# Pair scores as matmuls of 512 columns, with the halves of the sum added on VectorE

## What is computed

```python
scores = einsum('bsd,bmd->bsm', layernorm(x), ctx) / sqrt(1024)   # 8 x 1024 x 64
scores = where(mask, scores, -1e30)
x = x + where(any(mask), einsum('bsm,bmd->bsd', softmax(scores), ctx), 0)

y = layernorm(x)                                  # 8 x 1024 x 1024
base = einsum('btd,od->bto', y, weight)           # 1024 x 1024
probs = softmax(einsum('btd,ed->bte', y, router_w))     # 8 experts
w_dense = the two largest probs, normed to a sum of 1, zero elsewhere
Ax = einsum('nd,erd->ner', y, lora_A)             # rank 16
x = x + base + 2.0 * einsum('ner,ne,eor->no', Ax, w_dense, lora_B)
```

## Time and profile before

| | us |
|---|---|
| median of 3 runs | 981.63 |
| lowest and highest | 981.21, 981.75 |
| the profiled execution's own time | 982.01 |
| its span | 980.1 |

### The profile page before, as it was taken

One profiled execution on the slowest core, in us unless ns is written; L12 is line 12 of the kernel. 1 busy time (PEld: TensorE's weight loads), 2 busy tenths in 40 slices (PEclk: granted clock), 3 DMA queues, 4 the chain that ended last, 5 costly groups with the idle time before them and its releaser, 6 DMA issues.

```text
span 980.1 us, 18830 instructions
## 1 busy us (share of the span) xinstructions
PE 972.0 (99%) x6081; PEld 960.0 (98%) x6081; DVE 851.1 (87%) x2201; ACT 471.6 (48%) x930; POOL 141.2 (14%) x278
## 2 busy tenths in 40 slices
PE   8999999999999999999999999999999999999998
PEld 7999999999999999999999999999999999999998
DVE  6989988899988998989988899888999889888774
ACT  7755544445444455435444445454454444444420
POOL 3311111111111111111111111111111111111110
PEclk9999999999999999999999999999999999999999
DMA  8646666656576566575656665666765576665532
GB/s 323 230 130 156 160 169 161 186 137 161 151 177 188 146 130 157 162 203 150 162 127 158 202 159 154 140 154 176 178 151 158 124 192 167 161 161 125 123 71 71
DMA packets 156096, 156.62 MB, mean 160 GB/s; under 512 B 93968, under 2 KB 128912, under 8 KB 156048
## 3 DMA queue, kind: packets, MB, share of 16 engines
q1 hardware_dynamic: 137616, 138.63, 52.0%
q10 hardware_dynamic: 18432, 17.45, 9.5%
HBM read 78.74 MB, written 33.55 MB: 115 GB/s over the span
## 4 chain that ended last, share of the span: by engine, by line
PE 94%; DVE 3%; DMA 1%; issue 1%; ACT 1%; POOL 0%; SPq 0%; DVEq 0%; ACTq 0%; POOLq 0%
PE base_ps L1119 27%; PE base_ps L1120 27%; PE base_ps L1121 27%; PE ro_ps L1193 3%; PE ro_ps L1194 3%; PE s_ps L1148 3%; PE s_ps L1146 3%; PE base_ps L1225 1%; DMA xq<-xn 1%; DVE stats L913 1%; DVE x2T L929 0%; DVE w_raw L907 0%; DMA ctxT_raw<-in_ctxT 0%; DVE ctx_sum L790 0%; PE s_ps L1156 0%
## 5 line engine op out<-in xcount | busy, mean ns | idle before, releaser
L1119 PE MATMUL base_ps<-w_hi,xT_hi 128*128 128x392 f32 x1512 | 495.6, 328 | 0.8 <-DVE xT_lo L936 0.8
L1120 PE MATMUL base_ps<-w_lo,xT_hi 128*128 128x392 f32 x1512 | 494.4, 327 | 0.0
L1121 PE MATMUL base_ps<-w_hi,xT_lo 128*128 128x392 f32 x1512 | 494.4, 327 | 0.0
L1119 PEld LDWEIGHTS base_ps<-w_hi,xT_hi 128*128 128x128 f32 x1512 | 285.8, 189 | 2.8 <-issue 1.0
L1120 PEld LDWEIGHTS base_ps<-w_lo,xT_hi 128*128 128x128 f32 x1512 | 285.8, 189 | 1.6
L1121 PEld LDWEIGHTS base_ps<-w_hi,xT_lo 128*128 128x128 f32 x1512 | 285.8, 189 | 0.0
L929 DVE STREAM_TRANSPOSE x2T<-xq 128x512 f32<-128x512 f32 x122 | 166.5, 1472 | 18.1 <-DMA xq<-xn 18.0
L495 POOL TENSOR_TENSOR rstd<-var_eps,neg_half 128x1 f32<-128x1 f32 x64 | 61.7, 964 | 391.4 <-DVE var_eps L920 391.4
L622 ACT CAST xT_hi<-x2T 128x512 fp32r<-128x512 f32 x122 | 69.5, 617 | 99.0 <-DVE x2T L929 99.0
L936 DVE TENSOR_TENSOR xT_lo<-x2T,xT_hi 128x512 fp32r<-128x512 f32 x122 | 78.3, 683 | 0.0
L610 ACT ACTIVATE xn<-w_raw,shift,rstd 128x1024 f32<-128x1024 f32 x32 | 39.7, 1241 | 77.3 <-POOL shift L498 77.3
(11 more groups left out here) (132 smaller groups left out, 1389.8 us busy)
## 6 DMA issues: line engine op xcount, KB each, us to landing
xT_raw<-in_xT SPq DMA_DIRECT2D x62, 512.0 KB, 5.3
w_raw<-in_x SPq DMA_DIRECT2D x32, 512.0 KB, 3.5
out<-x_first SPq DMA_DIRECT2D x32, 512.0 KB, 2.9
out<-w_raw SPq DMA_DIRECT2D x31, 512.0 KB, 2.8
xq<-xn SPq DMA_DIRECT2D x122, 128.0 KB, 4.1
xq<-xn ACTq DMA_DIRECT2D x122, 128.0 KB, 4.1
x_first<-in_x SPq DMA_DIRECT2D x30, 512.0 KB, 3.6
h<-w_raw SPq DMA_DIRECT2D x248, 16.0 KB, 1.8
```

The lines of the kernel that those rows point to most:

```text
L1119: pe.matmul(out_, a_hi, w_h, start=start, stop=False, skip_group_check=again)
L1120: pe.matmul(out_, a_hi, w_l, start=False, stop=False, skip_group_check=again)
L1121: return pe.matmul(out_, a_lo, w_h, start=False, stop=stop, skip_group_check=again)
```

## The change

The scores' two matmuls per chunk become one: the moving operand is the high and the low part of both tiles, 512 columns, through `xT_parts`, and the result fills the whole bank `s_ps`, the products of the high part in its first half, those of the low part in its second. The two halves, which the accumulation in PSUM added before, are now added by VectorE: a VectorE operation is given only one operand in PSUM here, so ScalarE first copies the second half to `s_low` in SBUF, VectorE adds it to the first half into `s_sum`, and the transpose reads `s_sum`. The first tiles, whose scores go other ways (`first_scores`, `first_pair_scores`), stay as they are; 29 pairs are changed. Apart from that the loads of the next batch's context leave step 1: `load_ctxT` goes to step 0 and `load_ctx` to step 2.

```diff
@@ SyncE, step
-                if j == 1 and exists((b, TPB)):
+                if j == 0 and exists((b, TPB)):
+                    sp.wait_ge(ctxT_split, b + 1)
+                    load_ctxT(b + 1)
+                if j == 2 and exists((b, TPB)):
                     sp.wait_ge(ctx_split, b + 1)
                     sp.wait_ge(mask_step, b * 3 + 3)
                     load_ctx(b + 1)
-                    sp.wait_ge(ctxT_split, b + 1)
-                    load_ctxT(b + 1)
@@ ScalarE
+            def s_low_copy(tile):
+                act.wait_ge(sT_done, pairs(tile, 1, 1))
+                act.copy(s_low, s_ps[:, T2:2 * T2]).then_inc(s_low_copied, 1)
...
                 if h_is_late(tile):
                     hT_high(tile)
+                if j % 2 == 1 and exists(after(tile, 3)) and not turned_on_pe(after(tile, 3), 6):
+                    s_low_copy(after(tile, 3))
                 if exists(nxt):
                     x2T_high(nxt)
@@ VectorE, s_transposes
-                dve.wait_ge(sT_done, pairs(tile, 1, 1))
+                dve.wait_ge(s_low_copied, pairs(tile, 1, 1 - 3))
+                dve.tensor_tensor(s_sum, s_ps[:, 0:T2], s_low, ALU.add).then_inc(s_sum_done, 1)
+                dve.wait_ge(s_sum_done, pairs(tile, 1, 1 - 3))
                 dve.transpose(sq.rearrange("p (j k c) -> p k j c", k=2, c=QP),
-                              s_ps[:, 0:T2].rearrange("p (j c k) -> p k j c", k=2, c=QP)).then_inc(sq_done, 1)
+                              s_sum.rearrange("p (j c k) -> p k j c", k=2, c=QP)).then_inc(sq_done, 1)
@@ TensorE, pair_scores
                 for c in range(C):
-                    pe.matmul(s_ps[:, 0:T2], ctxT[:, c, :], xT_hi[:, :, c, :].rearrange("p t n -> p n t"),
-                              start=(c == 0), stop=False)
-                    mm = pe.matmul(s_ps[:, 0:T2], ctxT[:, c, :], xT_lo[:, :, c, :].rearrange("p t n -> p n t"),
-                                   start=False, stop=(c == C - 1))
+                    mm = pe.matmul(s_ps[:, :], ctxT[:, c, :], xT_parts[:, :, :, c, :].rearrange("p k t n -> p k n t"),
+                                   start=(c == 0), stop=(c == C - 1))
```

More of the change, by code:

```diff
@@ L196, in xattn_lora_moe_kernel @@
         sq = w_raw[0][:, C - 2, 0:T2]
+        s_sum = w_raw[0][:, C - 4, 0:T2]
+        s_low = w_raw[0][:, C - 5, 0:T2]
         s_raw = w_raw[0][:, C - 3, 0:T2].rearrange("p (i k c) -> p i k c", i=Q, k=2)
@@ L324, in xattn_lora_moe_kernel @@
         e_loaded = sem("e_loaded")
+        s_low_copied = sem("s_low_copied")
+        s_sum_done = sem("s_sum_done")
         sq_done = sem("sq_done")
```

## The result

| | before | after |
|---|---|---|
| median, range of 4 runs, us | 981.64 (981.21 to 981.75) | 995.92 (995.84 to 996.37) |
| profiled execution, its span | 982.01, 980.1 | 995.95, 994.2 |

The ratio is 1.0145, 95% interval 1.0133 to 1.0158. The change costs 14.3 us; 995.7 was forecast. The granted clock is 1.0 in both.

A forecast was written before the change was run, and what follows sets the result against it. TensorE, busy 99%, was taken as the bound, with little margin before its readouts. Matmuls -1.5, stalls +16.1, old waits -0.5 give +14.1 on 982.01: 996.1, or 995.7 us as median; range 987 to 1003.

The forecast's parts named there:

- The mechanism: From scores to next even readout, the path has 0.36 us margin; the added delay makes TensorE stall in 29 pairs.
- ordinary: 15 pairs at neither special place: path 13.42 against TensorE's 13.78; 0.54 us idle plus 0.10 restart each, 9.6 us.
- with the mean: 7 pairs in whose window TensorE also issues the context's mean: 0.31 us idle plus 0.10 restart each, 2.9 us.
- The first tiles of a batch: 7 pairs whose path ends at a new batch's first tile, VectorE about 0.1 late: 0.52 us each, 3.6 us.
- The delay itself: Copy and add move the transpose's start after the scores from +0.03 to +0.88, 0.85 us, all arriving at the path's end.
- rival 3: Unseen path slack, say where e transfers land: nothing waits, only -1.5 us stays, 980.1; decides at 0.5 slack; chance 0.08.
- The matmuls: Scores on TensorE: eight matmuls of 512 columns replace sixteen of 256, 0.05 us less in 29 pairs, -1.5 us.
- rival 4: The 512-column matmuls overlap at the skill's 131 ns: 20 us off TensorE with the same stalls, about 976; chance 0.02.
- The transpose: VectorE's transpose of the scores, reading SBUF instead of PSUM, was left equal; bound from above 0.27 us more.
- The loads: Context's loads moved to two even steps: taken at 0; gain at most 0.5 us, delaying transfers at most 4.3.
- the router's logits: At the even step VectorE waits for them anyway; its total wait for them was to grow.
- The cover of hT_lo: In ordinary odd steps hT_lo is done 1.13 us before TensorE uses it; 0.28 would be left after the delay.

The follow-up runs named there:

- e3: Changed kernel without ScalarE's copy and VectorE's addition, transpose taking the first half only; wide matmuls and moved loads stay: 981.63 us, ratio 0.9998 to the kernel before.
- e5: Kernel before with ScalarE's copy and VectorE's addition ahead of the transpose, 256-column matmuls and loads as before: 996.3 us, ratio 1.0145 to the kernel before.
- e13: Changed kernel with TensorE's even-step readout moved behind two rounds (one in one step) of the last product: 988.02 us, ratio 1.0067 to the kernel before.
- e4: Kernel before with one more VectorE addition of 128x256, result unused, ahead of the scores' transpose, which still reads PSUM: 985.61 us, ratio 1.0051 to the kernel before.
- e8: Changed kernel with the fourth e transfer of every even tile issued by ScalarE instead of SyncE: 999.22 us, ratio 1.0175 to the kernel before.
- e2: Changed kernel with the context's loads back in step 1, wide matmuls and sum kept: 996.66 us, ratio 1.0149 to the kernel before.
- e1: Kernel before with only the context's loads moved to steps 0 and 2: 981.72 us, ratio 0.9997 to the kernel before.
- e6: Changed kernel with VectorE's hT_low moved behind norm2_moments in the odd steps: 998.62 us, ratio 1.017 to the kernel before.

## Why the prediction was right, point by point

**The mechanism.** The margin of 0.36 us, the delay of more than twice that, and one stall for each of the 29 pairs were what happened. Taking the sum out takes the loss away (e3), and putting copy and add into the kernel before brings it (e5, 14.7 us). With copy and add as they are, another order on TensorE alone gives back more than half (e13), so it is not the work of VectorE and ScalarE as such that costs, but what TensorE waits for. That is shown.

**The sum.** Idle for each pair, forecast and measured: ordinary 0.54 against 14.30-13.78 = 0.52, first of a batch 0.42 against 0.52, with the mean 0.31 against 14.32-14.01 = 0.31. With 0.10 for each restart that makes 15 x 0.62 + 7 x 0.62 + 7 x 0.41 = 16.5, against 16.1. From readout to readout the timelines give 12.4 us more between an odd step's and the next even step's, where the stall lies, 1.1 in the other half, where the restart's 0.10 stands against the shorter scores, and 0.2 ahead of the first pair: 13.7 of the span's 14.1.

**What was luck in it.** That the forecast came within 0.3 us is partly luck. It took 13.42, the path of the last pair, for all ordinary pairs, whose mean is 13.50, and it let the whole delay of 0.85 arrive, of which 0.75 did. The two errors cancel: 14.27 forecast, 14.25 measured. Two sums don't come out as they stand. The steps to the transpose add up to +0.87 and not +0.88. And a delay between 0.7 and 1.1 gives 995.7-3.3 = 992.4 and, with the loads' collision, 995.7+5.5+4.3 = 1005.5, where 991 and 1003 are named; the measured time lies well inside either way.

**The first tiles of a batch.** They were put lower than the ordinary ones, as VectorE would be late at the scores already and a part of the delay would hide behind that. It did not: their transpose starts 0.98 after the scores where it was 0.13, as much added as in the ordinary pairs. A term of the sum that was 0.7 us too small.

**The delay itself.** From the scores' end to the transpose it was to be 0.88; it is 0.90 in the ordinary pairs. Before it was 0.04, so 0.86 were added, of which 0.75 arrive at eT (13.50 to 14.25). By the means of the 15 pairs 0.08 go between the start of the transpose and that of the readout's add, and 0.04 from there to the aggregate. The prediction's "nothing on the path waits for TensorE in between" is wrong: the readout's add did, by up to 0.13, as e4 shows. That "what is added in front of it arrives at its end" holds for nearly nine tenths of the change's delay, but for 0.26 of e4's 0.46. The old stalls were also more than the 0.5 taken off: TensorE's side of before exceeds 13.78 and 14.01 by 15 x 0.03 + 7 x 0.04 + 7 x 0.05 = 1.1 us. Both errors are small, and 16.5 - 1.1 - 1.5 = 13.9 is near the 13.7 that the timelines add up to.

**Hidden slack (rival 3).** It was looked for in the landing of the e transfers, and something of it is there: in e8 SyncE's last issue ends 0.67 earlier and eT comes no earlier. But rival 3 needed slack against a late xn, and there is hardly any: in the changed kernel xn is done 0.76 later than before and eT 0.75. Of the 0.5 us of hidden slack at which it would have decided, there are 0.13, at the readout's add. That a shorter issue would shorten the path, as I expected of e8, fell.

**The matmuls.** 1.73 us against 1.79 in the last pair, as expected, and no wide overlap (rival 4). In time the gain was not seen: e3 against before has 0.4 us, with 1.5 outside its interval, and e5 against e2 none. The -1.5 in the sum is seen in the trace only, as 1.65 us of shorter scores; in e3 part of it goes to other stalls. By the Trainium skill (TensorE: Matmul & The Clock Gate, Back-to-back issue gap) 512 columns in a stream would come at about 131 ns; these eight come at 1.73/8 = 216, so the trace disagrees, as it did before the change.

**The transpose.** Taken as equal. Its record is longer, 509 ns instead of 466. From its start to that of the next operation it is 931.22-930.79 = 0.43 in the last pair and 917.05-916.55 = 0.50 before, which looks like a gain, but the 0.50 is the wait for the readout. Where VectorE does not wait, the transpose from PSUM has 0.37 (e4) or 0.40 to 0.44 (the late pairs of before), and that from SBUF 0.40 to 0.46. By the Trainium skill (VectorE: DVE Perf Modes, the TRN2 errata section) a source in SBUF has 62 cycles less of fixed cost, by an estimate 65 ns: for this transpose the traces agree with it neither in the recorded durations (450 ns from PSUM in e4) nor from start to start.

**The loads.** Taken at nothing, and nothing it is: ratio 0.9997 alone (e1), and 1.0149 without them against 1.0145 with them (e2).

**Wrong: the router's logits.** VectorE's wait for them was to grow and fell, from 45.5 to 35.5 us. Its idle time in all is 980.1-851.1 = 129.0 before and 994.2-865.8 = 128.4 after: the copy, add and longer transpose fill what TensorE's stalls leave open, and the new wait for ScalarE's copy takes its share. I had added TensorE's stalls to the waits and left out VectorE's own new work. It moved no term of the sum.

**The cover of hT_lo.** The 0.28 us that were said to be left held: 3 waits, 0.9 us in the changed kernel. They are about all there is: e6 makes hT_lo 0.6 later, e13 lets the delay run on to it, and TensorE stalls there in place of the readout.

## What to carry to other kernels

Before adding work to an engine that looks half idle, follow the path from the operation in front of which it goes to the point where the bound engine next waits, and take TensorE's own work between the same points: the difference, here 0.3 us in 13.8, is what may be added for little, and a busy share of 99% with 1.3 us of waits doesn't show how small it is. Look also for operations on the path that wait for something else, as the readout's add did: they take up a part of what is added. Cost comes beyond the margin: 0.46 us in front cost 4.0 us in the kernel, the next 0.40 us cost 10.7. Moving an operation that seems to lie on the path (hT_lo, an issue) is worth trying only once the timeline shows that the next step starts when it ends. And behind such a path there can be others with margins of the same size, which take the stall over, as hT_lo's did here.

## What was not expected of the hardware

- A VectorE operation of 0.28 us between bn_stats and the aggregate costs nothing there: the aggregate starts 4.16 us after the scores with it and 4.18 without.
- The DMA group of two 128 KB and four 16 KB transfers takes 6.45 us from the first issue to the consumer, and 6.52 with one of six issues on another queue. SyncE's issue length isn't its bound.
- TensorE pays the restart without having idled: in e4 readouts that start the usual 0.16 after the matmul before them take 0.48 instead of 0.38 where eT was done only 0.06 earlier (305.28+0.30 to 305.64).
- The time from one operation's start to the next one's is not the operation's price if the next waits for something else: the transpose of 128x256 from PSUM shows 0.50 us before and 0.37 in e4.
- A transpose of 128x512 from PSUM in the order of these scores takes 732 ns, and that of xq from SBUF, of the same size with a strided pattern, 1472.
